# Two more pairs of router and LoRA extensions in a fused linear and mixture-of-LoRA kernel, with a longer x ring

## What is computed

```python
y      = x @ W.T + b + 2 * (x @ lora_A[slot[b]]) @ lora_B[slot[b]]   # rank 16, one adapter per batch
logits = y @ route_w.T                                               # 8 experts
weight = one_hot(top1(logits)) * top1_value
h      = y @ A.T                                                     # 8 experts x rank 16 = 128 columns
out    = x + (weight * h) @ Bw                                       # 128 -> 2048
```

## Time and profile before

| | us |
|---|---|
| three timed runs | 284.00, 284.53, 284.55 (median 284.53) |
| profiled execution, its own time | 284.19 |
| its span, first to last instruction | 282.4 |
| PE / PEld / DVE / ACT / POOL busy | 277.1 / 221.0 / 200.7 / 110.3 / 14.9 |
| granted TensorE clock, mean | 1.000 (2.4 GHz) |

### The profile page before, as it was taken

The page is one execution under the profiler, slowest core; times in us unless marked ns, Lnnn a source line. Parts: engine busy times, 40 slices in busy tenths (PEclk is TensorE's granted clock), DMA queues, the critical chain, the costliest instruction groups (busy, mean ns, idle before and its releaser), DMA issues.

```text
span 282.4 us, 4103 instructions
## 1 busy us (share of the span) xinstructions
PE 277.1 (98%) x1601; PEld 221.0 (78%) x1601; DVE 200.7 (71%) x223; ACT 110.3 (39%) x151; POOL 14.9 (5%) x46
## 2 busy tenths in 40 slices
PE   8999999999999999999999999999999999999993
PEld 5999999997773888888588758867885888588882
DVE  0033010177497889999889969996998799788794
ACT  0001011387684645534275346326533743370000
POOL 7600021000001000000000000000000000000000
PEclk9999999999999999999999999999999999999999
DMA  7999999999993034999966993999399859606688
GB/s 257 382 377 394 399 407 411 384 407 421 412 408 133 2 149 187 352 343 388 396 269 230 418 402 146 348 405 398 136 370 406 316 176 412 287 22 253 261 355 321
DMA packets 19590, 88.50 MB, mean 313 GB/s; under 512 B 2410, under 2 KB 4594, under 8 KB 12018
## 3 DMA queue, kind: packets, MB, share of 16 engines
q1 hardware_dynamic: 16272, 83.70, 76.1%
q10 hardware_dynamic: 3298, 4.54, 4.4%
HBM read 54.60 MB, written 33.55 MB: 312 GB/s over the span
## 4 chain that ended last, share of the span: by engine, by line
PE 93%; DVE 6%; issue 0%; DVEq 0%
PE bank_out L683 11%; PE bank_eh L811 11%; PE bank_eh L825 10%; PE bank_eh L840 10%; PE bank_out L749 9%; PE bank_out L772 9%; PE bank_out L763 9%; PE bank_eh L683 5%; PE bank_rl L683 5%; PE bank_rl L790 5%; PE bank_eh L790 5%; DVE x_ring L666 4%; PE bank_rl L721 1%; PE bank_eh L711 1%; PE bank_rl L845 1%; PE bank_eh L846 1%
## 5 line engine op out<-in xcount | busy, mean ns | idle before, releaser
L402 ACT ACTIVATE x_hi<-x_ring 128x1024 fp32r<-128x1024 f32 x64 | 67.4, 1061 | 57.7 <-PE bank_eh L840 57.3
L518 DVE TENSOR_TENSOR x_lo<-x_ring,x_hi 128x1024 fp32r<-128x1024 f32 x64 | 77.6, 1222 | 8.7 <-ACT x_hi L402 8.7
L607 DVE TENSOR_TENSOR x_ring<-bank_out,x_ring 128x1024 f32<-128x1024 f32 x54 | 65.9, 1220 | 2.9 <-PE bank_out L772 2.7
L811 PE MATMUL bank_eh<-x_hi,m_hi 128*128 128x512 f32 x128 | 50.6, 396 | 0.0
L825 PE MATMUL bank_eh<-x_lo,m_hi 128*128 128x512 f32 x128 | 49.9, 390 | 0.0
L840 PE MATMUL bank_eh<-x_hi,m_lo 128*128 128x512 f32 x128 | 49.8, 389 | 0.0
L749 PE MATMUL bank_out<-wh_hi,bw_hi 128*128 128x512 f32 x120 | 46.7, 389 | 0.0
L763 PE MATMUL bank_out<-wh_lo,bw_hi 128*128 128x512 f32 x120 | 46.7, 389 | 0.0
L772 PE MATMUL bank_out<-wh_hi,bw_lo 128*128 128x512 f32 x120 | 46.7, 389 | 0.0
L811 PEld LDWEIGHTS bank_eh<-x_hi,m_hi 128*128 128x128 f32 x128 | 24.0, 188 | 10.7 <-issue 5.9
L840 PEld LDWEIGHTS bank_eh<-x_hi,m_lo 128*128 128x128 f32 x128 | 24.0, 188 | 5.1
(11 more groups left out here) (99 smaller groups left out, 227.1 us busy)
## 6 DMA issues: line engine op xcount, KB each, us to landing
x_ring<-xT SPq DMA_DIRECT2D x32, 1024.0 KB, 8.4
outT<-x_ring SPq DMA_DIRECT2D x26, 1024.0 KB, 4.9
w_ring<-W SPq DMA_DIRECT2D x24, 512.0 KB, 10.6
w_ring<-W SPq DMA_DIRECT2D x14, 256.0 KB, 5.9
outT<-x_ring SPq DMA_DIRECT2D x5, 512.0 KB, 2.8
outT<-x_ring ACTq DMA_DIRECT2D x4, 512.0 KB, 2.8
outT<-x_ring SPq DMA_DIRECT2D x5, 256.0 KB, 2.7
x_ring<-loraB ACTq DMA_DIRECT2D x8, 128.0 KB, 9.9
```

Of the source, the lines that this page charges most:

```text
L402: act.activation(out, in_, ACT.Copy).then_inc(done, 1)
L518: dve.tensor_tensor(out, a, b, ALU.subtract).then_inc(done, 1)
L607: dve.tensor_tensor(x, out_bank(b, j)[:, :, :], x, ALU.add).then_inc(v_out, 1)
L811: mm(bank_h, m_hi[:, c, :], hi, start=(c == 0), stop=False)
```

## The change

- `TWINS` is now 2, 4 and 6 and `LATE` is 3 and 5 (batches counted from 0; counted from 1 these are batches 4 and 5, 6 and 7). Extensions 3 and 4 run back to back in unit 3, behind its step 1 and the output pair there, and 5 and 6 likewise in unit 5. Units 3, 4, 5 and 6 begin with their main step. Extension 7 stays at the start of unit 7.
- The wait for `weigh` of the unit that ends, which stood in the extension, now stands before the last matmul of the last output pair for units 3 to 6 as well.
- ACT and DVE fold extensions 3 (5) at step 2 and 4 (6) at steps 3 and 4. `split_lo(b + 1, 3)` goes behind `weigh` in units 3 and 5 as in unit 1, not in units 2, 4 and 6.
- The x ring has 14 slots, and SP issues `load_x(k - 1 + 14)` behind `store(k)`. To make room, `g_a`, `bp`, `pb_sum`, `ones` and `bias_sb` lie in slot 10, whose first load waits until they are used up; `lb`, `bw_raw`, `lb_cols` lie in slots 12, 13, 11.
- `la` holds one batch. ACT issues its loads one by one: batches 1 and 2 in the first part (behind the `g_a` transfers, and before the last `m_block`), batch b + 3 at the end of unit b, each behind POOL's copy of the one before.
- `e_top`, `e_two`, `e_sum` and `e_odd` share two tiles on different partitions, and the first of the two copies of `stack` is now the one that `split_e` reads.

The core of the diff:

```diff
-    XRING = 12
+    XRING = 14
...
+        TWINS = range(TWIN, NB - 1, 2)
+        LATE, LATE_AT = range(TWIN + 1, NB - 2, 2), 2
...
+                elif slot == WORK:
+                    sp.wait_ge(t_pb, 1)
+                    sp.wait_ge(v_glo, 3)
+                    sp.wait_ge(a_ghi, 6)
+                    sp.wait_ge(a_beats, 3)
...
-            LAG = 2
+            LAG = 1
...
+                pool.wait_ge(d_la, 16 * (b + 1))
                 if b >= 2:
                     pool.wait_ge(t_ext, b - 1)
-                pool.tensor_copy(ext[b % 2][:, :, E:E + R], la[:, b, :, :]).then_inc(g_ext, 1)
+                pool.tensor_copy(ext[b % 2][:, :, E:E + R], la[:, :, :]).then_inc(g_ext, 1)
...
+            def load_a(b):
+                if b >= 1:
+                    act.wait_ge(g_ext, b)
+                act.dma_start(la[:, :, :].rearrange("p c r -> p (c r)"),
+                              loraA[bass.ds(slot[b], 1), :, :].rearrange("s p n -> p (s n)")).then_inc(d_la, 16)
...
+                    if b in LATE and j == LATE_AT:
+                        sum_two(b)
+                        sum_all(b)
+                        split_e(b)
+                    if b in LATE and j == LATE_AT + 1:
+                        sum_two(b + 1)
+                    if b in LATE and j == LATE_AT + 2:
+                        sum_all(b + 1)
...
-                    elif b + 1 < NB and (b + 1, j) != (TWIN, NP2 - 1):
+                    elif b + 1 < NB and not (b + 1 in TWINS and j == NP2 - 1):
                         split_lo(b + 1, j - SRING)
...
-                    if (b, j, i) == (TWIN - 2, NP2 - 1, 1):
-                        pe.wait_ge(v_wh, TWIN)
+                    if (b + 2 in TWINS or b + 2 in LATE) and (j, i) == (NP2 - 1, 1):
+                        pe.wait_ge(v_wh, b + 2)
                     last = mm(out, bw_lo[:, o], hi, start=False, stop=True)
...
-                        if c == C - 1 and b > TWIN:
+                        if c == C - 1 and b > TWIN and b not in TWINS and b not in LATE:
                             pe.wait_ge(v_wh, b)
...
-                if b != TWIN:
+                if b not in TWINS and b not in LATE:
                     extension(b)
                 if b + 1 == TWIN:
-                    extension(TWIN)
+                    extension(b + 1)
...
+                    if b in LATE and j == LATE_AT - 1:
+                        extension(b)
+                        extension(b + 1)
```

More of the change, by code:

```diff
@@ L107, in adaln_ffn, with work @@
         x_ring = sb("x_ring", [P, XRING, PIECE])
-        lb = x_ring[:, 8, :].rearrange("p (b c r) -> p b c r", b=NB, c=C)
-        bw_raw = x_ring[:, 9, :]
+        lb = x_ring[:, 12, :].rearrange("p (b c r) -> p b c r", b=NB, c=C)
+        bw_raw = x_ring[:, 13, :]
         lb_cols = x_ring[:, 11, :].rearrange("p (c b r) -> p c b r", b=NB, c=C)
-        EARLY = (8, 9, 11)
+        EARLY = (11, 12, 13)
+        WORK = 10
+        def work(at, n, rows=P):
+            return x_ring[0:rows, WORK, at:at + n]
+        g_a = work(0, NB * XN, GROUP).rearrange("p (b n) -> p b n", b=NB)
+        bp = work(NB * XN, XN)
+        pb_sum = [work((NB + 1) * XN + i * PN, PN) for i in range(2)]
+        ones = work((NB + 1) * XN + 2 * PN, P)
+        bias_sb = work((NB + 1) * XN + 2 * PN + P, C)
+        assert (NB + 1) * XN + 2 * PN + P + C <= PIECE
         phase1 = ExitStack()
@@ L122, in adaln_ffn @@
         phase1.close()
[L123 to L126, removed]
+        e_pair = sb("e_pair", [P, T])
+        e_two, e_top = e_pair[0:HALF, :], e_pair[HALF:P, :]
+        e_side = sb("e_side", [P, T])
+        e_odd, e_sum = e_side[0:GROUP, :], e_side[2 * GROUP:3 * GROUP, :]
         wh_hi = [sb(f"wh_hi{i}", [P, T], F32R) for i in range(2)]
@@ L129, in adaln_ffn @@
         wh = sb("wh", [P, T])
[L130 to L136, removed]
+        assert (C - WO) * PN + NHEAD * (HEAD_W + HO * PN) + XN + 2 * E + P // 2 <= 7 * T, "the second lot covers the first"
+        e_st = sb("e_st", [P, T], F32R)
+        ahead = sb("ahead", [P, T], F32R)
+        e_bias = sb("e_bias", [P, 1])
         slots = sb("slots", [1, NB], I32)
+        sb("space", [P, HALF - 16])
         m_hi = sb("m_hi", [P, C, ER], F32R)
@@ L171, in adaln_ffn @@
         bank_out = [psum(f"bank_out{i}", [P, 2, T]) for i in range(2)]
-        d_slots, d_bias, d_bw, d_lb, d_la0, d_la = (sem(n) for n in ("d_slots", "d_bias", "d_bw", "d_lb", "d_la0", "d_la"))
+        d_slots, d_bias, d_bw, d_lb, d_la = (sem(n) for n in ("d_slots", "d_bias", "d_bw", "d_lb", "d_la"))
         d_pt = [sem(f"d_pt{i}") for i in range(NPT)]
@@ L479, in stack @@
                     act.wait_ge(t_stack, b)
+                copy(e_st[2 * GROUP:3 * GROUP, :], e_sum[:, :], a_ehi)
                 copy(e_st[0:GROUP, :], e_sum[:, :], a_ehi)
-                copy(e_st[2 * GROUP:3 * GROUP, :], e_sum[:, :], a_ehi)
             for b in range(NB):
-                if b != TWIN:
+                if b not in TWINS and b not in LATE:
                     top(b)
                 for j in range(NP2):
-                    if j == 0 and b != TWIN:
+                    if j == 0 and b not in TWINS and b not in LATE:
                         odd(b)
@@ L490, in _ @@
                         stack(b)
-                        top(TWIN)
+                        top(b + 1)
                     if b + 1 == TWIN and j == 1:
[L493 to L496, removed]
+                        odd(b + 1)
+                    if b in LATE and j == LATE_AT:
+                        top(b)
+                        odd(b)
+                        stack(b)
+                    if b in LATE and j == LATE_AT + 1:
+                        top(b + 1)
+                    if b in LATE and j == LATE_AT + 2:
+                        odd(b + 1)
+                    if b + 1 in TWINS and j == TWIN_AT:
+                        stack(b + 1)
+                    if j == EHI_AT and b not in TWINS and b + 1 not in TWINS:
                         stack(b)
@@ L510, in _ @@
                 copy(wh_hi[b % 2][:, :], wh[:, :], a_wh)
+                if b + 3 < NB:
+                    load_a(b + 3)
             for j in range(0, NP2 - 1, 2):
@@ L627, in _ @@
                         split_e(b)
-                        sum_two(TWIN)
+                        sum_two(b + 1)
                     if b + 1 == TWIN and j == 1:
-                        sum_all(TWIN)
-                    if j == ELO_AT and b not in (TWIN - 1, TWIN):
+                        sum_all(b + 1)
+                    if b in LATE and j == LATE_AT:
+                        sum_two(b)
+                        sum_all(b)
+                        split_e(b)
+                    if b in LATE and j == LATE_AT + 1:
+                        sum_two(b + 1)
+                    if b in LATE and j == LATE_AT + 2:
+                        sum_all(b + 1)
+                    if j == ELO_AT and b not in TWINS and b + 1 not in TWINS:
                         split_e(b)
@@ L646, in _ @@
                     weigh(b)
-                if b + 1 == TWIN:
-                    split_e(TWIN)
+                if b + 1 in TWINS:
+                    split_e(b + 1)
                     weigh_lo(b)
@@ L654, in _ @@
                     add_held(C - 3)
-                if b + 1 == TWIN:
-                    split_lo(TWIN, NP2 - 1 - SRING)
+                if b + 1 in TWINS:
+                    split_lo(b + 1, NP2 - 1 - SRING)
                 else:
@@ L742, in out_pair @@
                     pe.wait_ge(v_whlo, b + 1)
-                ext_next = b + 2 if j == NP2 - 1 and TWIN < b + 2 < NB else None
+                if j == 0 and b + 1 in LATE:
+                    ext_next, ext_last = b + 1, b + 2
+                elif j == NP2 - 1 and TWIN < b + 2 < NB and b + 2 not in TWINS and b + 2 not in LATE:
+                    ext_next = ext_last = b + 2
+                else:
+                    ext_next = None
                 hi, lo = wh_hi[b % 2][:, :], wh_lo[b % 2][:, :]
```

31 lines of the change are left out of this document (10 added, 21 removed).

## The result

| | before | changed |
|---|---|---|
| median of the timed runs, us (runs) | 284.04 (10) | 285.10 (10) |
| lowest and highest | 283.34, 284.55 | 284.52, 285.57 |
| profiled execution, us | 284.19 | 285.00 |
| its span, us | 282.4 | 283.2 |

The medians are 1.06 us apart. The ratio of the runs is 1.0032, with a 95% interval from 1.0020 to 1.0044: slower by 0.9 us (0.6 to 1.2). The forecast was 1.0 us and 285.4. A later comparison (e8) gave 1.0059 (1.0040 to 1.0077), 1.7 us. One of the four executions of e6 (293.27 us at a mean granted clock of 0.982) was in a slower state and is left out of its ratio.

What follows compares the result with a forecast made beforehand. TensorE, 93% of the span, was taken as the bound. From the profiled 284.19, - 0.68 + 1.70 gave 285.21, or 285.55 from the median; the forecast was 285.4 us, slower by 1.0, with eight in ten between 284.2 and 286.6.

Steps and rivals of the forecast that it cites:

- The pairs' gain: Two new extension pairs, in units 3 and 5: each saves TensorE 0.34 us, -0.68 us together.
- The stall at the ends of units 2 and 4: TensorE waits for weigh before the last output matmul: 0.85 us each (0.75 to 0.94), +1.70 us together.
- The second reason: Ends of units 2 and 4: weigh hangs on TensorE's last main step; an empty VectorE gains at most 0.1 us.
- The ends of units 3 and 5: weigh precedes split_lo there; load 0.08 us late, taken as 0, or 0.6 us each if the cover is gone.
- The fold: Folding extensions 3 and 5: a chain of about 4.2 us within 7.5 us; cost 0, cover 3 us.
- Transfers: Extension 4 needs x piece 19 earlier, in unit 3; landing forecast at 143.7, cost 0, cover 3 us.
- LoRA A: First part: loads of batches 1 and 2 arrive in time, the second issued at 68.2 in ScalarE's 0.35 us wait; cost 0.
- A: The pairs win: weigh is in time at units 2 and 4, only -0.68 us remains, 283.85 us; chance 0.12.
- B: The two terms about cancel: the stall is only some 0.35 us each, 284.5 us; chance 0.14.
- C: More waits: units 3 and 5 up to 0.6 us each, or piece 19 or last M block late; 286.5 to 288; chance 0.14.
- D: A pair in mid-unit pays the change of form as two singles do, saving nothing: 286.2 us; chance 0.08.
- E: Stalls halve the granted clock for part of a unit, 5 to 20 us more, above 290 us; chance 0.01.

Runs made afterwards that it cites:

- e8: The changed kernel as it is, timed again; ratio to the kernel before 1.0059.
- e6: The changed kernel with the pairs (3, 4) and (5, 6) at the very start of units 3 and 5; ratio 1.0178.
- e10: The kernel of e7 once more; ratio 0.9974, stretch (start of pair (1, 2) to start of extension 7) 156.33 us.
- e3: The changed kernel without the two new pairs, keeping ring of 14, earlier loads, moved tiles and single LoRA buffer; ratio 0.9997, stretch 157.04 us.
- e2: The kernel before with only the wait for weigh added before the last output matmul of units 2 and 4; ratio 1.0058.
- e1: The changed kernel with weigh before the last x_lo split in units 2 and 4 too; 283.56 us, ratio 0.9984.
- e4: The changed kernel with VectorE's x additions in units 2 and 4 cut to 64 of 512 tokens, order kept; ratio 1.0042.
- e7: The kernel of e1 with the split of step 6 also behind weigh in units 3 and 5; ratio 0.9983.

## Why the prediction was right, and where its sum was off

- **The pairs' gain.** Costed 0.34 us each; 0.36 measured (e10 against e3). Right, in mid-unit too.
- **The stall at the ends of units 2 and 4.** Costed 0.85, between 0.75 and 0.94; 0.86 in the matmuls' starts, 0.86 in e2's stretch, 0.90 by e1 against the changed kernel. Right, with its reason: e1 takes it away by order alone, e4 shows that the load on VectorE is worth nothing there. The way from the release to the 0.85 was misread, though, and came out by luck. I took the matmul at 267.48 in the earlier trace rows for one that its late load had held up. But the matmul before it began at 267.25, so 267.48 was its turn. The first section on the hardware below has what the rows show.
- **The second reason.** I gave an empty VectorE up to 0.1 us; e4 shows 0.
- **The ends of units 3 and 5, the mis-sized term.** I took 0: a load 0.08 us late, covered by 0.1. The load waited 0.25 us, its turn was 0.21 late (165.63 for 165.42), and the end cost 0.10 at the next matmul, 0.15 by e7 against e1. `weigh` ended at 165.57 (164.88 + 0.69), 0.15 us after the load's turn, where I had reckoned 0.03 after it. The mechanism was the one named, two small sums (L588 and L594) in steps 3 and 4 against the gaps there, and the size between my two ends (0 and 0.6). In unit 3 VectorE has no gap left from step 3 on, but for the 0.1 us in front of `weigh` that stands in unit 1 too:

```profile
150.23 1.23 DVE L541 TENSOR_TENSOR x_lo<-x_ring,x_hi 128x1024 fp32r<-128x1024 f32 x1 [2.00 <-ACT x_hi L414]
...
152.62 0.68 DVE L588 TENSOR_TENSOR e_pair<-bank_eh,e_pair 64x512 f32<-64x512 f32 x1
...
155.73 0.68 DVE L594 TENSOR_TENSOR e_side<-e_pair,e_side 32x512 f32<-32x512 f32 x1
...
164.88 0.69 DVE L619 TENSOR_TENSOR wh<-bank_eh,wh 128x512 f32<-128x512 f32 x1
```

- **The sum.** -0.72 + 1.73 + 0.30 = +1.31; the stretch says +1.37. The forecast had -0.68 + 1.70 + 0 = +1.02. The run times (+0.9 and +1.7) lie on both sides. That the first of them came within 0.1 us of the forecast is luck: the sum was 0.35 short of the stretch, 0.30 of it the ends of units 3 and 5.
- **The fold.** Cost 0, right: from the end of extension 3 (144.02) to the end of `split_e` (148.23) it took the 4.2 us reckoned, with 2.15 us of VectorE waiting at its head, and TensorE waited for none of it.
- **Transfers.** Cost 0: e3 shows it for the ring, and in the changed kernel no weight load waits for an x piece. But one wait was missed: slot 5's new load also waits until its store has landed (issued at 127.95, landed 7.4 us later). SP issued the load of piece 19 at 135.34, 1.6 us after `store(6)` let it through. It landed 8.1 us later, at 143.4 (forecast 143.7), so the cover of some 3 us stood. The second pair had less: piece 27 was issued at 187.80 and landed 10.0 us later, at 197.8, and extension 6 (from 197.17) wants it for its last quarter, near 199.7, which leaves 1.9 us. e6 shows what is covered: its pairs want these pieces some 5 us earlier, and their weight loads wait 2.3 and 2.9 us.
- **LoRA A.** The loads of batches 1 and 2 landed 6.8 and 6.9 us after their issue (8.2 in the earlier trace rows), and the second was issued at 63.09, not at 68.2, so the 0.35 us that I had laid into ScalarE's gap was not needed at all.
- **The rivals.** A (the pairs win) would have been right with another order: e1, with `weigh` first in units 2 and 4, gains 0.43 us in the stretch, and A's full 0.68 needs e7's order too (0.73). B would have needed a stall of 0.35; C was there as a mechanism, with 0.15 and not 0.6 us, and my own sign for it (the load waits at the end of units 3 and 5) came true. D and E (in the changed kernel) did not occur.

## What to carry over

When a step that covered a wait is moved, read from the old trace when the event that is waited for happens, and not only whether it was waited for: here `weigh` had been late all along, 0.9 us behind the place where its wait would land, under 3.3 us of cover. Then look at what stands ahead of that event on its own engine: a split that hangs on TensorE's last main step made `weigh` late however empty VectorE was. With `weigh` in front of it in units 2 and 4, a loss of 1.4 us in the stretch became a gain of 0.4, and of 0.7 with the ends of units 3 and 5 set right too. And choose for such small steps a stretch of the trace that holds the change and little of the scatter; it told e1 and e7 apart by 0.3 us, which twelve runs of each did not.

## What I had not expected of the hardware

- **In three places a late weight load cost the matmuls its lateness less 0.11 us.** The rows of the kernel before, around those of the earlier trace rows:

```profile
267.03 0.19 PEld L751 LDWEIGHTS bank_eh<-wh_hi,bw_lo 128*128 128x128 f32 x1
267.25 0.39 PE L751 MATMUL bank_eh<-wh_hi,bw_lo 128*128 128x512 f32 x1
...
267.72 0.40 PE L749 MATMUL bank_eh<-wh_hi,bw_hi 128*128 128x512 f32 x1
```

  The waiting load began at 267.38, 0.12 after its turn (267.03 + 0.23). Its matmul began at its own turn, and the one behind it at 267.72, 0.01 late. In the changed kernel the loads were 0.21 and 0.97 late, and the matmul behind the waiting one 0.10 and 0.86. In all three the second matmul begins 0.33 to 0.34 us after the waiting load. With a long wait, load and matmul are both recorded at 135.83, the matmul lasts 0.50 instead of 0.39, and the next starts 0.33 later instead of 0.23. So the prediction's 0.15 from release to matmul was too long for a long wait by 0.09, and the follower's 0.10, which it did not have, made up for it. The Trainium skill says in "TensorE: Matmul & The Clock Gate" (Architectural detail: the array is 16× 32×32, not 1× 128×128) that a matmul can begin before its weight load completes; these rows agree (both at 135.83, with a load of 0.19 us), and show that the matmul behind it pays.
- **ScalarE's issue of a transfer runs ahead of its queued work.** The load of batch 2 stands behind four x_hi conversions in ScalarE's order; its issue is recorded before them (changed kernel, one case):

```profile
62.85 0.38 ACT L414 ACTIVATE m_hi<-bank_out 128x256 fp32r<-128x256 f32 x1
63.09 0.34 ACTq L410 DMA_DIRECT2D la<-loraA  x1
63.13 0.25 ACT L414 ACTIVATE ext<-bank_out 128x16 f32<-128x16 f32 x2
63.41 3.90 ACT L414 ACTIVATE x_hi<-x_ring 128x1024 fp32r<-128x1024 f32 x4
```

- **The granted clock fell behind one late x piece and not behind the other.** In e6 it was 1.00 in the 6 us from 143 us on, behind the first (the weight loads idle for 2.33 us, the matmuls for 1.42). Behind the second (2.89 and 1.99) it was 0.50 from 199 to 202 us, with matmuls at half speed. There is one case of each, so what decides it is not shown. Around the 1.0 us stall at the end of unit 2 in the changed kernel it stayed at 1.00.
